# Causal attention with a gated LoRA branch on one core: minus the row maximum goes into the score bank ahead of the matmuls, output scaling moves to VectorE, and the jobs stand in another order

## The chip, the core and the metric

The program runs on one core of a Trainium2 chip. Five engines work in it, each with its own list of instructions, in order, tied together by semaphores: TensorE (PE, with the weight loads shown apart as PEld), VectorE (DVE), ScalarE (ACT), GpSimd (POOL) and SyncE (SP, which only issues DMAs here). The metric is the device time of one execution in microseconds (us), as the median of several runs.

## What is computed

The input x is 2048 tokens by 256. After a layer norm there are two branches, and the result is x + attention * silu(ffn). Everything is fp32.

```python
k, q, v = (einsum('ihd,bpd->biph', W, x) for W in (W_K, W_Q, W_V))   # 16 heads of 128
scores  = einsum('biph,biqh->biqp', k, q)                            # causal
masked  = scores * mask - 1e10 * (1 - mask)
attn    = softmax(masked / sqrt(128), axis=-1)
z       = einsum('biqp,biph->biqh', attn, v)
out     = einsum('df,bqf->bqd', W_O, z_flat)
# ffn: x W_base + b + 2 * (one of 8 LoRA experts, picked by argmax of a router)
```

## The kernel before

**Precision.** Each fp32 product is three matmuls in a fast fp32 form: hi*hi, hi*lo and lo*hi (`mm3`, lines 304 to 308). So every operand is held as a high part and a rest. The high part is written by ScalarE (a copy that rounds), the rest by VectorE (a subtraction).

**Tiling.** The queries of a head form 4 blocks of 512 (g = 0 to 3). A score tile is 128 keys by 512 queries, keys on the partitions. Block g has 4 (g + 1) such tiles, the last four of them on the diagonal and so 512, 384, 256 and 128 wide. That makes 40 tiles for a head, 80 for a pair of heads and 640 in all: 448 of the full width and 64 of each smaller width together with them (64 diagonal ones of full width are among the 448). Score banks in PSUM are used in turn, three of them; three more (`aux`) serve all other products.

**One tile.** PE computes the scores, adds the mask on a diagonal tile by one bf16 matmul (line 763), and then minus the row maximum is added. The maximum of a query is a number for each column of this layout, so it cannot be an activation's bias. There are two ways:

- a fourth matmul (line 765) of a matrix of ones with `shift`, a 128 x 512 tile in which POOL has put minus the maxima on diagonals (line 431);
- where `on_vector` is true (256 of the 640 tiles: blocks 2 and 3, not on the diagonal, five of six), a VectorE addition on the bank (line 620) of `negmax`, the same product made once for the block by the job Spread (a matmul at line 750 and a VectorE copy at line 610).

ScalarE then writes exp twice from the bank: `probs` (line 517) and its high part `p_hi` (line 518). VectorE writes `p_lo` (line 581). POOL sums the tiles into `colsum` (lines 456 to 463). PE multiplies with the values (the job Value).

**Row maxima.** For each block PE computes the scores a second time, the other way round and from the high parts alone (RowMax, line 745), 640 times; VectorE reduces each (lines 595 and 601), and then the four or more partial maxima (line 606).

**Output.** When a block's z is full, ScalarE and VectorE split it, PE takes the sums of the 512 queries (line 789) and multiplies with W_O (Out). ScalarE scales a 128 x 256 piece of that by 1 / sum into `scaled`, which is part of `gate` (line 527), and POOL adds it to `acc` (line 447). There are 256 such pieces.

**Order.** The order of all jobs is one list that the five engines share. A table `SCHEDULE` of 80 pieces, one for each score tile of a pair of heads, says which jobs follow that tile: P for a projection, V for a value projection, M for a RowMax, B for Spread, v or w for a Value, Z, S and O for the steps of the output. Each engine goes through the same list and takes its part of every job. SP loads the weights of the next head or pair once POOL has split the last ones (lines 347 to 376).

## Time and profile before

| what | number |
|---|---|
| median of 3 runs | 1572.15 us (1568.87 to 1574.76) |
| the profiled execution, its own time | 1567.74 us |
| its span (first to last instruction) | 1565.9 us |
| granted TensorE clock, mean | 0.986 of full speed |
| PE busy | 1507.5 us, 96% |
| DVE busy | 1297.8 us, 83% |
| POOL busy | 1118.6 us, 71% |
| ACT busy | 870.4 us, 56% |

Busy is the union of an engine's instructions. Matmuls are pipelined: the profile gives a 128 x 512 matmul some 0.4 us, while the next one starts 0.23 us after it. What a matmul takes from the engine is therefore read from the distance between two starts, not from its mean duration; the same is so, to a smaller extent, for ACT and DVE.

### The profile page before, as it was taken

To read this page: it belongs to the slowest core of one execution; us is meant where nothing else is said; L and a number is where in the kernel's file an instruction comes from. 1 tells how busy PE (TensorE), PEld (TensorE's weight loads), DVE (VectorE), ACT (ScalarE), POOL (GpSimd) and SP (SyncE) were. 2 spreads that over 40 slices of the span, in tenths; PEclk is the share of its full clock that TensorE was granted. 3 is DMA by queue.
4 is the path that set the end of the run, shared out by engine and by line. 5 is a ranking of instruction groups with operands and counts; after the bars stand their busy time and mean duration, and the time that the engine had idled before them with its cause. 6 is when DMAs were issued, how large, how long until landed. Compare 5 with 4: busy or idle time off the path is not lost.

```text
span 1565.9 us, 24075 instructions
## 1 busy us (share of the span) xinstructions
PE 1507.5 (96%) x8192; PEld 1271.6 (81%) x8192; DVE 1297.8 (83%) x2701; ACT 870.4 (56%) x1812; POOL 1118.6 (71%) x1010
## 2 busy tenths in 40 slices
PE   4999999999999999999999999999999999999987
PEld 3788878888888887888788888888888887888765
DVE  6788987889789796888978898897978989788864
ACT  2456555565555564566555655565655665566541
POOL 3468876687677786778866876778867788668860
PEclk9899999999999999999999999999999999999998
DMA  2000000000000000000000000000000000000002
GB/s 87 15 1 1 14 1 14 1 8 8 1 14 1 15 1 8 8 1 14 1 15 0 8 8 1 14 1 8 8 1 14 1 8 1 18 1 0 1 27 81
DMA packets 11640, 16.87 MB, mean 11 GB/s; under 512 B 768, under 2 KB 7424, under 8 KB 11520
## 3 DMA queue, kind: packets, MB, share of 16 engines
q1 hardware_dynamic: 11520, 15.35, 3.1%
q8 instruction: 66, 1.08, 0.3%
q14 instruction: 54, 0.44, 0.1%
HBM read 13.25 MB, written 2.10 MB: 10 GB/s over the span
## 4 chain that ended last, share of the span: by engine, by line
PE 76%; DVE 14%; POOL 5%; issue 3%; DMA 1%; ACT 0%; SPq 0%; POOLq 0%; DVEq 0%
PE ps L306 21%; PE ps L308 20%; PE ps L307 20%; DVE p_lo L581 7%; PE ps L745 6%; PE ps L765 4%; DVE ps L620 3%; PE ps L789 2%; DVE partmax L595 2%; POOL colsum L463 2%; PE ps L763 1%; POOL acc L447 1%; POOL shift L431 1%; POOL wo_hi L396 1%; POOL wo_lo L399 1%
## 5 line engine op out<-in xcount | busy, mean ns | idle before, releaser
L463 POOL TENSOR_TENSOR colsum<-colsum,probs 128x512 f32<-128x512 f32 (+3 forms) x512 | 628.8, 1228 | 194.6 <-ACT probs L517 158.6
L581 DVE TENSOR_TENSOR p_lo<-probs,p_hi 128x512 fp32r<-128x512 f32 (+3 forms) x640 | 589.6, 927 | 44.5 <-issue 31.7
L517 ACT ACTIVATE probs<-ps 128x512 f32<-128x512 f32 (+3 forms) x640 | 342.8, 536 | 481.7 <-PE ps L765 252.3
L518 ACT ACTIVATE p_hi<-ps 128x512 fp32r<-128x512 f32 (+3 forms) x640 | 339.8, 531 | 0.0
L447 POOL TENSOR_TENSOR acc<-acc,gate 128x256 f32<-128x256 f32 x256 | 235.0, 938 | 86.1 <-ACT gate L527 85.2
L595 DVE TENSOR_REDUCE partmax<-ps 128x1 f32<-128x512 f32 x384 | 250.4, 679 | 22.9 <-PE ps L745 22.8
L306 PE MATMUL ps<-qT_hi,kT_hi 128*128 128x512 f32 (+3 forms) x640 | 236.1, 369 | 0.0
L306 PE MATMUL ps<-p_hi,v_hi 128*128 128x512 f32 (+3 forms) x640 | 232.9, 364 | 2.7 <-DVE p_lo L581 2.7
L745 PE MATMUL ps<-kT_hi,qT_hi 128*128 128x512 f32 (+3 forms) x640 | 224.8, 378 | 10.9 <-DVE partmax L595 8.9
L308 PE MATMUL ps<-qT_hi,kT_lo 128*128 128x512 f32 (+3 forms) x640 | 234.3, 366 | 0.0
L307 PE MATMUL ps<-qT_lo,kT_hi 128*128 128x512 f32 (+3 forms) x640 | 234.3, 366 | 0.0
L307 PE MATMUL ps<-p_lo,v_hi 128*128 128x512 f32 (+3 forms) x640 | 232.9, 364 | 0.0
L308 PE MATMUL ps<-p_hi,v_lo 128*128 128x512 f32 (+3 forms) x640 | 232.8, 364 | 0.0
L620 DVE TENSOR_TENSOR ps<-ps,negmax 128x512 f32<-128x512 f32 x256 | 176.5, 689 | 17.4 <-PE ps L308 14.7
L745 PEld LDWEIGHTS ps<-kT_hi,qT_hi 128*128 128x128 f32 x640 | 121.2, 191 | 43.7 <-DVE partmax L595 23.2
L765 PE MATMUL ps<-shift,ones_r 128*128 128x512 f32 (+3 forms) x384 | 152.2, 396 | 0.0
L306 PEld LDWEIGHTS ps<-p_hi,v_hi 128*128 128x128 f32 x640 | 121.3, 189 | 20.3 <-DVE p_lo L581 5.4
L308 PEld LDWEIGHTS ps<-qT_hi,kT_lo 128*128 128x128 f32 x640 | 121.1, 189 | 19.6
L459 POOL TENSOR_TENSOR colsum<-probs 128x384 f32<-128x384 f32 (+1 forms) x64 | 78.3, 1223 | 81.3 <-ACT probs L517 81.3
L308 PEld LDWEIGHTS ps<-p_hi,v_lo 128*128 128x128 f32 x640 | 120.6, 188 | 18.9
L307 PEld LDWEIGHTS ps<-qT_lo,kT_hi 128*128 128x128 f32 x640 | 121.1, 189 | 17.1
L527 ACT ACTIVATE gate<-ps,rinv 128x256 f32<-128x256 f32 x256 | 109.4, 475 | 45.0 <-PE ps L308 39.0
(114 smaller groups left out, 2636.4 us busy)
## 6 DMA issues: line engine op xcount, KB each, us to landing
wraw<-wqk_dram SPq DMA_DIRECT2D x16, 256.0 KB, 2.6
acc<-x_dram SPq DMA_DIRECT2D x4, 512.0 KB, 7.3
wraw<-wv_dram SPq DMA_DIRECT2D x8, 256.0 KB, 2.7
wraw<-wo_dram SPq DMA_DIRECT2D x8, 256.0 KB, 2.7
probs<-x_dram SPq DMA_DIRECT2D x4, 512.0 KB, 4.6
out_dram<-acc SPq DMA_DIRECT2D x4, 512.0 KB, 3.1
wraw<-ffn_w_dram SPq DMA_DIRECT2D x2, 196.0 KB, 2.4
wraw<-lora_b_dram SPq DMA_DIRECT2D x1, 128.0 KB, 2.7
```

The source lines that it names most:

```text
L306: nc.tensor.matmul(dst, w_hi, m_hi, start=first, stop=False)
L307: nc.tensor.matmul(dst, w_hi, m_lo, start=False, stop=False)
L308: return nc.tensor.matmul(dst, w_lo, m_hi, start=False, stop=last)
L447: nc.gpsimd.tensor_tensor(dst, dst, scaled[:, k, :], ALU.add).then_inc(out_added, 1)
L463: nc.gpsimd.tensor_tensor(total[:, c0:], total[:, c0:], tile[:, c0:], ALU.add)\
L517: nc.scalar.activation(probs[:, k, c0:], src, ACT.Exp, scale=SCALE).then_inc(probs_ready, 1)
L518: nc.scalar.activation(p_hi[:, k, c0:], src, ACT.Exp, scale=SCALE).then_inc(hi_ready, 1)
L581: nc.vector.tensor_tensor(p_lo[:, k, c0:], probs[:, k, c0:], f32(p_hi[:, k, c0:]), ALU.subtract)\
L595: nc.vector.reduce_max(dst, src, axis=AX).then_inc(aux_free, 1)
L620: nc.vector.tensor_tensor(bank, bank, negmax[:, job.g - 2, :], ALU.add)\
L745: nc.tensor.matmul(dst[:, 0:w], qT_hi[:, job.g, job.q * P:(job.q + 1) * P], kT_hi[:, k_slot(job.head, job.c), 0:w], start=True, stop=True)\
L765: op = nc.tensor.matmul(dst, ones_r[:, :], shift[:, job.g, :, :].rearrange("p t n -> p (t n)")[:, c0:], start=False, stop=True)
```

## The change

The three ways in which minus the maximum reached the scores are gone (`shift` on POOL, the matmuls at lines 750 and 765, the VectorE addition at line 620 and the copy at line 610). In their place:

- SP writes a block's `rowmax` (128 x 4) to DRAM and reads it back as one row of 512 on all 128 partitions, `maxrow`. Each of the two DMAs is waited for. The second also waits until the same block of the head before has used up its `maxrow`. SP now goes through the shared list, with the weight loads between these.
- ScalarE writes `-maxrow` into the score bank two tiles ahead (`seed`), and PE's three matmuls add to it (`start=False`). For that the banks' accumulate marks are set once by 12 matmuls at the start. PE's wait on the exp of three tiles before is replaced by a wait for the seed.
- The row that arrives is in the order 4 p + t, so the seed reads it with a step of four floats.
- VectorE scales and adds an output piece in one instruction; ScalarE and POOL have no part in it any more.
- `SCHEDULE` is another table.

```diff
-            def make_shift(job, block_no):
-                pool.wait_ge(max_ready, block_no)
-                k = job.g
-                nc.gpsimd.tensor_tensor(
-                    shift[:, k, :, :], neg_ident[:, None, :].broadcast_to([P, TB, P]),
-                    rowmax[:, k, :][:, :, None].broadcast_to([P, TB, P]), ALU.mult).then_inc(shift_ready, 1)
...
+                if isinstance(job, RowMax) and job.last:
+                    blocks += 1
+                    row = max_dram[job.head * NB + job.g]
+                    sp.wait_ge(max_ready, blocks)
+                    sp.dma_start(row.rearrange("(p t) -> p t", t=TB), rowmax[:, job.g, :]).then_inc(max_out, 16)
+                    sp.wait_ge(max_out, 16 * blocks)
+                    if job.head:
+                        sp.wait_ge(seeded, tiles_until((job.head - 1) * NB + job.g))
+                    sp.dma_start(maxrow[:, job.g, :], row.partition_broadcast(P)).then_inc(max_spread[job.g], 16)
...
+            def seed(job):
+
+                if job.n >= SCORE_BANKS:
+                    act.wait_ge(hi_ready, job.n - SCORE_BANKS + 1)
+                if job.kt == 0:
+                    act.wait_ge(max_spread[job.g], 16 * (job.head + 1))
+                q = columns(job) // P
+                nc.scalar.activation(st[job.n % SCORE_BANKS].rearrange("p (t n) -> p t n", t=TB)[:, q:, :],
+                                     maxrow[:, job.g, :].rearrange("p (n t) -> p t n", t=TB)[:, q:, :],
+                                     ACT.Copy, scale=-1.0).then_inc(seeded, 1)
...
                     nc.scalar.activation(probs[:, k, c0:], src, ACT.Exp, scale=SCALE).then_inc(probs_ready, 1)
                     nc.scalar.activation(p_hi[:, k, c0:], src, ACT.Exp, scale=SCALE).then_inc(hi_ready, 1)
-                elif isinstance(job, Out):
...
+                    if n + SEED_AHEAD < len(scores):
+                        seed(scores[n + SEED_AHEAD])
...
-                    if on_vector(job):
...
-                        dve.wait_ge(scores_ready, job.n + 1)
-                        nc.vector.tensor_tensor(bank, bank, negmax[:, job.g - 2, :], ALU.add)\
-                          .then_inc(shifted, 1)
...
+                        op = nc.vector.scalar_tensor_tensor(
+                            dst, aux[job.aux % AUX_BANKS][:, k * D:(k + 1) * D],
+                            rinv[:, job.gi % 2, q:q + 1], dst, ALU.mult, ALU.add)
+                    op.then_inc(aux_free, 1)
...
+            for bank in st:
+                for q in range(TB):
+                    op = nc.tensor.matmul(bank[:, q * P:(q + 1) * P], ones_r[:, :], ones_r[:, :], start=q == 0,
+                                          stop=True, skip_group_check=True)
+            op.then_inc(bits_set, 1)
...
-                    if job.kt == 0:
-                        pe.wait_ge(shift_ready, job.head * NB + job.g + 1)
-                    if n >= SCORE_BANKS:
-                        pe.wait_ge(hi_ready, n - SCORE_BANKS + 1)
+                    pe.wait_ge(seeded, n + 1)
...
-                    if not on_vector(job):
-                        op = nc.tensor.matmul(dst, ones_r[:, :],
-                                              shift[:, job.g, :, :].rearrange("p t n -> p (t n)")[:, c0:],
-                                              start=False, stop=True)
...
-    "V11 w | w V01 V00 | w | Pk02 Pq03 V10 v z7 s7 | "
+    "V00 w Pq03 V01 w w z7 | | Pk02 | s7 Pk03 v V11 | o70 v M0222 | M0212 o71 v M0202 M0232 v | V21 S0 Z0 | v V10 "
...
```

**TensorE, around two narrow diagonal tiles.** Names: `ps<-qT_hi,kT_hi` and the two rows after it are a score tile, `ps<-mask_bf,ident_bf` the mask, `ps<-shift,ones_r` minus the maximum, `ps<-kT_hi,qT_hi` a RowMax, `ps<-p_hi,v_hi` and the two after it a Value. Before, in block 1 of an odd head:

```order
L306 MATMUL ps<-qT_hi,kT_hi 128x256 [waits hi_ready]
L307 MATMUL ps<-qT_lo,kT_hi 128x256
L308 MATMUL ps<-qT_hi,kT_lo 128x256
L763 MATMUL ps<-mask_bf,ident_bf 128x128
L765 MATMUL ps<-shift,ones_r 128x256
L306 MATMUL ps<-p_hi,v_hi 128x512 [waits lo_ready]
L307 MATMUL ps<-p_lo,v_hi 128x512
L308 MATMUL ps<-p_hi,v_lo 128x512
L745 MATMUL ps<-kT_hi,qT_hi 128x512 [waits aux_free] x2
```

The same tile of the same kind of block now, from the end of the tile before it (384 wide) to the start of the one after it (128 wide):

```order
L731 MATMUL ps<-mask_bf,ident_bf 128x128
L719 MATMUL ps<-kT_hi,qT_hi 128x512 [waits aux_free]
L281 MATMUL ps<-qT_hi,kT_hi 128x256 [waits seeded]
L282 MATMUL ps<-qT_lo,kT_hi 128x256
L283 MATMUL ps<-qT_hi,kT_lo 128x256
L731 MATMUL ps<-mask_bf,ident_bf 128x128
L281 MATMUL ps<-p_hi,v_hi 128x512 [waits lo_ready]
L282 MATMUL ps<-p_lo,v_hi 128x512
L283 MATMUL ps<-p_hi,v_lo 128x512
L281 MATMUL ps<-qT_hi,kT_hi 128x128 [waits seeded]
```

The matmul of ones with `shift` is gone, the tile waits for `seeded`, and the jobs between two tiles are others.

**ScalarE, at the same place.** `probs` and `p_hi` are the two exps of a tile, `kT_hi` and `z_hi` copies for other jobs, `gate` the scaling of an output piece, `ps<-maxrow` a seed. Before:

```order
L506 ACTIVATE kT_hi<-ps 128x512 [waits aux_full]
L517 ACTIVATE probs<-ps 128x512 [waits sum_done,scores_ready]
L518 ACTIVATE p_hi<-ps 128x512
L517 ACTIVATE probs<-ps 128x384 [waits sum_done,scores_ready]
L518 ACTIVATE p_hi<-ps 128x384
L527 ACTIVATE gate<-ps,rinv 128x256 [waits out_added,aux_free,aux_full]
L527 ACTIVATE gate<-ps,rinv 128x256 [waits out_added]
```

Now:

```order
L486 ACTIVATE kT_hi<-ps 128x512 [waits aux_full]
L498 ACTIVATE probs<-ps 128x384 [waits sum_done,scores_ready]
L499 ACTIVATE p_hi<-ps 128x384
L478 ACTIVATE ps<-maxrow 128x128 [waits hi_ready]
L498 ACTIVATE probs<-ps 128x256 [waits sum_done,scores_ready]
L499 ACTIVATE p_hi<-ps 128x256
L478 ACTIVATE ps<-maxrow 128x512 [waits max_spread2,hi_ready]
L498 ACTIVATE probs<-ps 128x128 [waits sum_done,scores_ready]
```

Every tile has a third instruction, which fills the bank of the tile two further on; the first tile of a block also waits for the DMA there. The scalings of outputs are gone.

**VectorE, just before that place.** `ps<-ps,negmax` is the addition to a score bank, `acc<-ps,rinv,acc` the new scaling and adding. Before:

```order
L620 TENSOR_TENSOR ps<-ps,negmax 128x512 [waits scores_ready]
L581 TENSOR_TENSOR p_lo<-probs,p_hi 128x512 [waits hi_ready]
L595 TENSOR_REDUCE partmax<-ps 128x1 [waits aux_full] x2
L638 MEMSET wait_slot 128x1 [waits out_scaled]
L581 TENSOR_TENSOR p_lo<-probs,p_hi 128x512 [waits hi_ready]
```

Now:

```order
L566 TENSOR_REDUCE partmax<-ps 128x1 [waits aux_full]
L551 TENSOR_TENSOR p_lo<-probs,p_hi 128x512 [waits hi_ready]
L603 SCALAR_TENSOR_TENSOR acc<-ps,rinv,acc 128x256 [waits aux_free,aux_full]
L603 SCALAR_TENSOR_TENSOR acc<-ps,rinv,acc 128x256
L551 TENSOR_TENSOR p_lo<-probs,p_hi 128x512 [waits hi_ready]
```

VectorE no longer stands between PE and ScalarE in any tile, and has two new instructions for each output job.

## Rows read from the trace of the kernel before

**Rows 1.** The page's busy times: busy us, share, count.
```profile
PE 1507.5 (96%) x8192; PEld 1271.6 (81%) x8192; DVE 1297.8 (83%) x2701; ACT 870.4 (56%) x1812; POOL 1118.6 (71%) x1010
```

**Rows 2.** Busy time by stretch: length, PE, PEld, DVE, ACT, POOL, clock, DMA.
```profile
80.00:1500.00 1420.00, 1398.82 (x7669) 1185.45 (x7668) 1211.87 (x2494) 827.46 (x1734) 1072.07 (x947) 1.00 0.02 6
```

**Rows 3.** Waits of the whole span: us in total, times, longest.
```profile
PEld ps L745 <- DVE partmax L595: 23.2, 38, 1.0
PE ps L750 <- POOL shift L431: 10.5, 8, 3.0
PE ps L745 <- DVE partmax L595: 8.9, 16, 0.7
```

**Rows 4.** PE in order of time: start, duration; width 512.
```profile
702.88 0.40 PE L765 MATMUL ps<-shift,ones_r 128*128 128x512 f32 x1
703.12 0.40 PE L306 MATMUL ps<-xT_hi,wqk_hi 128*128 128x512 f32 x1
```

**Rows 5.** The same, around a diagonal tile of width 256.
```profile
773.64 0.28 PE L308 MATMUL ps<-qT_hi,kT_lo 128*128 128x256 f32 x1
773.76 0.23 PE L763 MATMUL ps<-mask_bf,ident_bf 128*128 128x128 bf16 x1
773.80 0.36 PE L765 MATMUL ps<-shift,ones_r 128*128 128x256 f32 x1
774.00 0.39 PE L745 MATMUL ps<-kT_hi,qT_hi 128*128 128x512 f32 x1
```

**Rows 6.** Groups of instructions by shape: count, busy us, mean ns, idle before.
```profile
L581 DVE TENSOR_TENSOR p_lo<-probs,p_hi 128x512 fp32r<-128x512 f32 x448 | 447.3, 1000 | 40.1 <-issue 27.4 <-ACT p_hi L518 12.7
L447 POOL TENSOR_TENSOR acc<-acc,gate 128x256 f32<-128x256 f32 x256 | 235.0, 938 | 86.1 <-ACT gate L527 85.2
L620 DVE TENSOR_TENSOR ps<-ps,negmax 128x512 f32<-128x512 f32 x256 | 176.5, 689 | 17.4 <-PE ps L308 14.7
L527 ACT ACTIVATE gate<-ps,rinv 128x256 f32<-128x256 f32 x256 | 109.4, 475 | 45.0 <-PE ps L308 39.0 <-POOL acc L447 2.8
L431 POOL TENSOR_TENSOR shift<-neg_ident,rowmax 128x512 fp32r<-128x512 f32 x64 | 84.7, 1323 | 13.3 <-DVE rowmax L606 12.7
L765 PE MATMUL ps<-shift,ones_r 128*128 128x512 f32 x192 | 82.6, 430 | 0.0
L601 DVE CUSTOM_DVE_ANT_0 gate<-ps,mask_rows 128x256 f32<-128x256 f32 x64 | 26.6, 416 | 2.3 <-issue 2.3
L610 DVE COPY negmax<-ps 128x512 f32<-128x512 f32 x32 | 21.8, 682 | 4.0 <-PE ps L750 4.0
L750 PE MATMUL ps<-shift,ones_r 128*128 128x512 f32 x32 | 13.2, 414 | 10.5 <-POOL shift L431 10.5
```

**Rows 7.** The same view, the high part's exp on ACT, widest and narrowest.
```profile
L518 ACT ACTIVATE p_hi<-ps 128x512 fp32r<-128x512 f32 x448 | 266.4, 595 | 0.0
...
L518 ACT ACTIVATE p_hi<-ps 128x128 fp32r<-128x128 f32 x64 | 18.0, 281 | 0.0
```

**Rows 8.** ACT in order of time.
```profile
706.72 0.60 ACT L517 ACTIVATE probs<-ps 128x512 f32<-128x512 f32 x1 [0.45 <-PE ps L765]
707.21 0.59 ACT L518 ACTIVATE p_hi<-ps 128x512 fp32r<-128x512 f32 x1
```

**Rows 9.** DVE in order of time.
```profile
733.05 0.68 DVE L581 TENSOR_TENSOR p_lo<-probs,p_hi 128x512 fp32r<-128x512 f32 x1
...
734.43 1.26 DVE L581 TENSOR_TENSOR p_lo<-probs,p_hi 128x512 fp32r<-128x512 f32 x1
```

**Rows 10.** POOL in the same stretch.
```profile
733.85 2.99 POOL L463 TENSOR_TENSOR colsum<-colsum,probs 128x512 f32<-128x512 f32 x2 [0.69 <-ACT probs L517]
```

**Rows 11.** DMA issues of the page: count, KB each, median us to landing.
```profile
wraw<-wqk_dram SPq DMA_DIRECT2D x16, 256.0 KB, 2.6
wraw<-bias_dram SPq DMA_DIRECT2D x1, 128.0 KB, 3.5
```

More of the change, by code:

```diff
@@ L34 @@
 SCORE_BANKS = 3
+SEED_AHEAD = 2
 AUX_BANKS = 3
@@ L48 @@
 Normed = namedtuple("Normed", "aux ev c b")
-Spread = namedtuple("Spread", "aux head g")
 Base = namedtuple("Base", "b")
@@ L60, in number @@
             ev += 1
-        elif kind in (RowMax, Spread, Sums, Out):
+        elif kind in (RowMax, Sums, Out):
             plan.append(kind(aux, *args))
@@ L153, in follow @@
                 which = (code[1], head) if what == "P" else (head,)
-                kinds.append(({"P": Project, "M": RowMax, "B": Spread}[what], (*which, *digits[1:])))
+                kinds.append(({"P": Project, "M": RowMax}[what], (*which, *digits[1:])))
     for n, step in enumerate(steps):
@@ L162, in plan_program @@
     return number(mark_last(kinds))
-def on_vector(score):
-    return score.g >= 2 and score.kt < TB * score.g and score.kt % 6 > 0
 def attention_layer(nc, x, wqk, wv, wo, ffn_w, lora_b, bias, out):
@@ L283, in k_slot @@
             return NB + b if head % 2 and b < 2 else b
-        shifts_before = [0]
-        for job in plan:
-            if isinstance(job, Score):
-                shifts_before.append(shifts_before[-1] + on_vector(job))
-        SLOTS = 2
-        def tiles_out(job):
-            return job.gi * TB + 2 * job.half
+        scores = [job for job in plan if isinstance(job, Score)]
         def columns(t):
@@ L362, in _, with weights @@
-            for i in range(PAIRS - 1):
-                loads(i, False)
-            loads(PAIRS - 1, True)
-            sp.wait_ge(wqk_ready, H)
-            sp.wait_ge(wv_ready, PAIRS)
-            sp.wait_ge(wo_ready, PAIRS)
-            for c in range(DC):
-                sp.dma_start(wraw[:, c, 0:FW], ffn_w[:, c, :]).then_inc(ffn_in, 16)
-            sp.dma_start(wraw[:, 2, 0:D], lora_b).then_inc(ffn_in, 16)
-            sp.dma_start(wraw[:, 2, D:2 * D], bias.partition_broadcast(P)).then_inc(ffn_in, 16)
+            def weights(raw, src, nth, ready, count, arrived):
+                sp.wait_ge(ready, count)
+                sp.dma_start(wraw[:, raw, :], src[:, nth, :]).then_inc(arrived, 16)
@@ new lines, in ffn_weights @@
+            def ffn_weights():
+                sp.wait_ge(wqk_ready, H)
+                sp.wait_ge(wv_ready, PAIRS)
+                sp.wait_ge(wo_ready, PAIRS)
+                for c in range(DC):
+                    sp.dma_start(wraw[:, c, 0:FW], ffn_w[:, c, :]).then_inc(ffn_in, 16)
+                sp.dma_start(wraw[:, 2, 0:D], lora_b).then_inc(ffn_in, 16)
+                sp.dma_start(wraw[:, 2, D:2 * D], bias.partition_broadcast(P)).then_inc(ffn_in, 16)
+            blocks = 0
+            for job in plan:
+                if isinstance(job, RowMax) and job.last:
[7 more added lines that the diff above has]
+                    sp.dma_start(maxrow[:, job.g, :], row.partition_broadcast(P)).then_inc(max_spread[job.g], 16)
+                if not isinstance(job, Score):
+                    continue
+                i, at, last = job.n // TILES, job.n % TILES, job.n // TILES == PAIRS - 1
+                if at == 0:
+                    weights(0, wqk, 2 * i + 1, wqk_ready, 2 * i + 1, wqk_in)
+                if at == 1 and not last:
+                    weights(1, wv, i + 1, wv_ready, i + 1, wv_in)
+                if at == 10 and not last:
+                    weights(2, wo, i + 1, wo_ready, i + 1, wo_in)
+                if at == 12 and not last:
+                    weights(0, wqk, 2 * i + 2, wqk_ready, 2 * i + 2, wqk_in)
+                if at == 12 and last:
+                    ffn_weights()
@@ L499, in _ @@
             nc.scalar.activation(rstd[:, 1, :], rstd[:, 0, :], ACT.Sqrt).then_inc(sqrt_done, 1)
-            sums_aux = {job.gi: job.aux for job in plan if isinstance(job, Sums)}
+            def seed(job):
[7 more added lines that the diff above has]
+                                     ACT.Copy, scale=-1.0).then_inc(seeded, 1)
             for job in plan:
@@ L509, in _ @@
                     k = n % PROBS
-                    if on_vector(job):
-                        act.wait_ge(shifted, shifts_before[n] + 1)
-                    else:
-                        act.wait_ge(scores_ready, n + 1)
+                    if n == 0:
+                        act.wait_ge(bits_set, 1)
+                        for ahead in scores[:SEED_AHEAD]:
+                            seed(ahead)
+                    act.wait_ge(scores_ready, n + 1)
                     if n >= PROBS:
@@ L582, in lo_part @@
                   .then_inc(lo_ready, 1)
-            waiting, spread_out = [], None
+            sums_aux = {job.gi: job.aux for job in plan if isinstance(job, Sums)}
+            waiting = []
             for job in plan:
```

95 lines of the change are left out of this document (26 added, 69 removed), and 22 rows, old and new, of the table SCHEDULE.

## The prediction, made before the changed kernel was run

> **What bounds the kernel now.** I read the page's busy times first, then the busy times by stretch, then the waits, and then PE in order of time. The busy times put PE at 1507.5 of 1565.9 us, with DVE at 83%, POOL at 71% and ACT at 56% [rows 1]. Between 80 and 1500 us, which is nearly all of the work on the 640 tiles, PE is idle for 1420 - 1398.82 = 21.2 us [rows 2]. So PE is the bound, and a matmul less is time less, as long as nothing new makes PE wait. The waits show who makes it wait today: the Spread matmul for POOL's `shift`, 10.5 us, and RowMax matmuls for VectorE to empty an `aux` bank, 8.9 us on PE and 23.2 us on its weight loads [rows 3].
>
> How long a matmul holds PE has to be read between two starts. The matmul with `shift` starts at 702.88 and the next one at 703.12: 0.24 us, with a duration of 0.40 [rows 4]. Over many such pairs I use 0.233. For a diagonal tile of width 256 the score matmul takes 773.76 - 773.64 = 0.12, the mask 0.04, and the matmul with `shift` 774.00 - 773.80 = 0.20 [rows 5], which is 0.08 more than its width. I put these 0.08 down to the bf16 mask ahead of it, so they stay with the mask.
>
> **What goes from PE.** The matmuls at line 765: 192 of full width at 0.233, 44.7 us [count in rows 6], and 64 each of 384, 256 and 128 columns. For 256 I take 0.12 [rows 5], for 384 the middle between 0.12 and 0.233, 0.176, for 128 half of 0.12: 64 x (0.176 + 0.12 + 0.06) = 22.8 us. The 32 at line 750: 32 x 0.233 = 7.5 us [rows 6]. Together 75.0 us. If the 0.08 went too, on 256 diagonal tiles, it would be 20.5 us more. The durations of the same groups (82.6 us for the 192 alone) would make it nearly twice as much; they overlap, and I do not use them. The 12 matmuls at the start are issued while PE has nothing to multiply yet: its first work is a transpose that needs the layer norm. Cost 0.
>
> The Spread job goes, and with it the wait for POOL, 10.5 us [rows 3]. What is late next there? Nothing on PE: the maxima now come to ScalarE.
>
> **What goes from and comes to VectorE.** It loses 176.5 us (line 620) and 21.8 us (line 610) [rows 6]. It gets 256 pieces of 128 x 256, from PSUM and SBUF to SBUF. No such instruction is in the trace. The nearest row is the masked maximum of the same size, which also reads one operand from each: 0.416 [rows 6], so 106 us; the lower bound is half of a 512-wide one, 256 x 0.34 = 88, the upper one the p_lo rate of a 512-wide one halved, 256 x 0.5 = 128. Net -92 us. There is a second gain that the diff does not name. `p_lo` takes 0.68 us where POOL is idle and 1.26 us where POOL's sum stands beside it [rows 9, 10]; its mean is 1.00 [rows 6]. That is (1.00 - 0.68) x 448 = 143 us of waiting for POOL. POOL loses 235.0 and 84.7 us [rows 6] of its 1118.6, 29%, so some 0.29 x 143 = 41 us of it should go. VectorE falls from 1298 to about 1165 us, still some 79% of a shorter span. Since it is quicker, the waits of RowMax for an `aux` bank should shrink. Of 8.9 us and 23.2 us of late weight loads [rows 3] I take 6 us as gain; bounds 0 and 20.
>
> **What comes to ScalarE.** 640 seeds, from SBUF to PSUM. The nearest row is `p_hi` of the same size: 0.595 us for 512 columns, 0.281 for 128 [rows 7], so 266.4 + 18.0 and two widths between, about 340 us; back to back the next instruction starts 0.49 us after (706.72 to 707.21) [rows 8], which makes the lower bound about 0.8 of that, 275 us. It loses 109.4 us (line 527) [rows 6]. ScalarE ends between 870 - 109 + 275 = 1036 and 1101 us, under 75% of the new span. As a sum this fits. The seed's step of four floats is in no row of this trace. The upper bound is the slowest elementwise row of 512 columns, POOL's 1.32 [rows 6].
>
> Here a rule speaks against the change. The rows say nothing of a strided read on ScalarE. The Trainium skill, "SBUF — State Buffer", section on the DMA ports, says that SBUF has 16-byte lines, that full rate needs at least two accesses in a row to the same line, and that each access to a new line pays. A step of four floats touches a new line with each element. The page gives no price; no run here shows it yet. It is the first rival below.
>
> **Does the seed make PE wait?** Before, a tile waited for the exp of the third tile before it. Now it waits for its seed, which stands behind the exp of the second tile before it. From the end of one tile's scores to the start of the tile after the next, ScalarE must do two exps and a seed: the start of the first is 0.2 us behind (the pipelined end), then 0.49 + 0.49 + 0.60 = 1.8 us in all. What PE does in that time stands in the order. The tightest full-width places have only a Value job in each of the two gaps: 3 + 3 + 3 matmuls, 9 x 0.233 = 2.1 us, 0.3 to spare. The tightest narrow place is the one shown of PE: a RowMax 0.23, three matmuls of 256 at 0.12 and the mask with its 0.12, a Value 0.70, together 1.4; ScalarE needs 0.2 + two exps of 384 and a seed of 128. By the durations between 0.6 and 0.28 that is 0.2 + 0.4 + 0.4 + 0.28 = 1.3. So room everywhere, with very little in ten or so of the 80 pieces, and an average of about 3 us. Behind the seed stand the copies and exps of the next tiles, for which VectorE and PE wait; several tight tiles in a row leave ScalarE behind by some tenths. I take 1 us for each of the 8 pairs of heads, 8 us; bounds 0 and 40.
>
> **Are the maxima there in time?** From the last RowMax of a block: VectorE empties its queue and reduces, about 1.5 us, a DMA of 2 KB, a DMA of 256 KB. The weight loads of 256 KB land after 2.6 us, the broadcast of the bias after 3.5 [rows 11]. I take 2.6 + 3.5 and 0.5 us for each issue, 8.6 us in all. In the new table the last RowMax stands 5 to 12 tiles ahead of the block's first tile, and at the tightest places (six tiles, or seven, with little between) the matmuls of the pieces between add up to 9.3 to 10.6 us. POOL's `shift` took 1.3 us for that [rows 6] with four or five tiles. It fits, by 1 or 2 us. ScalarE can be held up ahead of that seed for a moment with its next exp behind it; that is in the 8 us.
>
> **The sum.** 1565.9 - 75.0 - 10.5 - 6 + 8 = 1482.4 us of span. The profiled execution took 1.8 us more than its span, and the median of the runs was 4.4 us above the profiled one: 1488.6, say 1488.
>
> **Rivals.**
> - *Slow seeds.* If the strided read runs at half the rate of the elements, a full seed takes 0.60 + 512 x (0.595 - 0.281) / 384 = 1.02 us. ScalarE then needs 2.2 us where the tight places give 1.9 to 2.1, eleven of 80 by the order: 88 x 0.25 = 22 us directly, and its load goes to 1101 + 190 = 1290 us, 85%, with queues behind it for as much again: 1535. For: no row has the access. Against: nothing but the page's rule.
> - *Very slow seeds, slower than before.* ScalarE becomes the bound once it would be busy for more than about 90% of 1566 us, that is 1410 us, of which 761 are its other work: 650 us of seeds, or 1.15 us for a full one. At POOL's 1.32 the full seeds make 591 us and the narrow ones about 150: 761 + 741 = 1502 us busy, and with the idle ends and 7% of waiting in order about 1640. It is slower from 1.15 us a seed.
> - *The maxima come late.* The way through DRAM needs to take 11 us instead of 8.6: then the tight blocks, two or three of eight in a pair, wait 1 to 2 us each, 8 x 2.5 x 1.5 = 30 us more: 1518. To be slower than before it would need 13 us.
> - *More is won.* The 0.08 behind each mask go with the `shift` matmul (20.5 us) and half of the late weight loads too (10 us more): 1457.
> - *The change does not do what it says* would be the case if the accumulate marks cost something on each tile; the same three matmuls run in both, so I give it nothing of its own.
>
> **How the numbers follow.** My forecast, 1488 with its own range 1465 to 1515: 0.66. More is won, 1457: 0.12. Slow seeds, 1535: 0.08. Late maxima, 1518: 0.06. Very slow seeds, 1640: 0.08. The rule on lines bears on the two kinds of slow seeds; it carries half of their 0.16. Half a per cent is what runs of this kernel can tell from no change. Faster takes the first four but for a fifth of the slow seeds: 0.90; within half a per cent 0.02; slower 0.08. The range for 8 in 10 is 1452 to 1535.
>
> **What would show it.** Right: PE starts after a score tile without the `shift` matmul, PE still over 93% busy, its distances between starts unchanged; seeds of 0.6 us; few waits of PE for ACT's seed; `p_lo` near 0.91 in the mean; VectorE near 1165 us. Wrong: a group of waits of PE on the seeds or of ACT on the maxima's DMA of tens of us; a seed above 0.9 us; diagonal tiles whose next matmul starts without the 0.08.

## The result: 1.4% faster, a quarter of the forecast

| | median us | runs |
|---|---|---|
| before | 1573.45 | 1568.87 to 1578.76 |
| after | 1548.33 | 1547.73 to 1548.76 |

The ratio is 0.9863, with an interval of 0.9824 to 0.9903 (the two medians of the table alone give 0.984). The gain is clear of the noise and under 2%. The forecast was 1488 us, with a range of 1452 to 1535, so the measured time lies above the range.

The changed kernel's page, first the busy times, which answer to [rows 1], then the chain that ended last by engine:

```profile
span 1546.2 us, 23204 instructions
...
PE 1459.5 (94%) x7788; PEld 1193.2 (77%) x7788; DVE 1248.1 (81%) x2541; ACT 1274.0 (82%) x2196; POOL 793.4 (51%) x688
...
PE 51%; ACT 24%; DVE 13%; issue 9%; POOL 2%; DMA 0%; SPq 0%; ACTq 0%; POOLq 0%; DVEq 0%
```

The same chain in the kernel before:

```profile
PE 76%; DVE 14%; POOL 5%; issue 3%; DMA 1%; ACT 0%; SPq 0%; POOLq 0%; DVEq 0%
```

ScalarE is at 1274 us, where I had 1036 to 1101, and has a quarter of the chain; before it had none of it. PE lost 404 matmuls, and is idle more. The middle stretch (length, then PE, PEld, DVE, ACT, POOL, clock) answers to [rows 2]:

```profile
80.00:1480.00 1400.00, 1345.26 (x7215) 1102.61 (x7214) 1158.51 (x2319) 1212.15 (x2094) 753.70 (x635) 1.00 0.08 18
```

PE is idle for 54.7 of 1400 us, against 21.2 of 1420. That is not all the time it stands late: a 512-wide matmul counts as busy for 0.40 us while the next can start after 0.23, so a short delay hides in the busy time. Counted by starts instead (each matmul at the median distance to the next for its width, those behind a mask apart), the matmuls themselves fall from 1457.0 to 1386.4 us, and what is left of the span rises from 108.9 to 159.8 us. Groups of instructions by shape (busy us, mean ns, idle before) show why:

```profile
L478 ACT ACTIVATE ps<-maxrow 128x512 f32<-128x512 f32 x448 | 517.5, 1155 | 8.9 <-DMA maxrow<-max_dram 8.7
L551 DVE TENSOR_TENSOR p_lo<-probs,p_hi 128x512 fp32r<-128x512 f32 x448 | 509.3, 1141 | 42.1 <-ACT p_hi L499 41.1
...
L603 DVE SCALAR_TENSOR_TENSOR acc<-ps,rinv,acc 128x256 f32<-128x256 f32 x256 | 111.3, 475 | 13.0 <-PE ps L283 12.1
```

A full seed takes 1.155 us. In order of time, ScalarE with the seed between its neighbours, which answers to [rows 8]:

```profile
700.61 0.61 ACT L499 ACTIVATE p_hi<-ps 128x512 fp32r<-128x512 f32 x1
701.08 1.14 ACT L478 ACTIVATE ps<-maxrow 128x512 f32<-128x512 f32 x1
702.10 0.63 ACT L504 ACTIVATE z_hi<-ps 128x512 fp32r<-128x512 f32 x1
```

The exp holds ScalarE for 701.08 - 700.61 = 0.47 us, the seed for 1.02. The waits, which answer to [rows 3], have new names:

```profile
PEld ps L281 <- ACT ps L478: 46.5, 106, 1.2
...
PEld ps L281 <- DVE partmax L566: 32.6, 31, 1.9
...
PEld ps L281 <- DVE p_lo L551: 25.1, 40, 1.3
PE ps L281 <- DVE partmax L566: 22.6, 23, 1.5
...
PE ps L281 <- DVE p_lo L551: 12.2, 16, 1.0
...
PE ps L281 <- ACT ps L478: 9.6, 32, 0.8
...
ACT ps L478 <- DMA maxrow<-max_dram: 8.7, 3, 8.2
```

Only part of the idle time names the seed. The rest names VectorE: what ScalarE hands on late (`p_hi`, the copies for `qT`, `kT`, `v` and z) VectorE finishes late, and PE waits there (read from the waits here; e13 below, where only the seed differs, bears it out). A slow engine that stands two steps back shows under the name of the step between.

### The profile page after: what moved, and what is told of

It reads as the page before. It is cut to its first block, busy times and chain, and to the rows that moved or that the text cites. A ratio compares the mean times of both kernels' runs of the same rounds, so it can differ in the third digit from the quotient of the medians.

```text
span 1546.2 us, 23204 instructions
## 1 busy us (share of the span) xinstructions
PE 1459.5 (94%) x7788; PEld 1193.2 (77%) x7788; DVE 1248.1 (81%) x2541; ACT 1274.0 (82%) x2196; POOL 793.4 (51%) x688
## 4 chain that ended last, share of the span: by engine, by line
PE 51%; ACT 24%; DVE 13%; issue 9%; POOL 2%; DMA 0%; SPq 0%; ACTq 0%; POOLq 0%; DVEq 0%
PE ps L281 15%; PE ps L282 14%; PE ps L283 14%; ACT ps L478 7%; ACT probs L498 7%; ACT p_hi L499 6%; DVE p_lo L551 6%; PE ps L719 4%; DVE partmax L566 3%; POOL colsum L433 2%; PE ps L754 2%; ACT qT_hi L486 1%; DVE z_lo L588 1%; ACT z_hi L504 1%; PE ps L731 1%
## 5 line engine op out<-in xcount | busy, mean ns | idle before, releaser
L433 POOL TENSOR_TENSOR colsum<-colsum,probs 128x512 f32<-128x512 f32 (+3 forms) x512 | 610.2, 1192 | 388.3 <-ACT probs L498 373.6
L478 ACT ACTIVATE ps<-maxrow 128x512 f32<-128x512 f32 (+3 forms) x640 | 645.3, 1008 | 8.9 <-DMA maxrow<-max_dram 8.7
L551 DVE TENSOR_TENSOR p_lo<-probs,p_hi 128x512 fp32r<-128x512 f32 (+3 forms) x640 | 614.9, 968 | 42.4 <-ACT p_hi L499 41.4
L498 ACT ACTIVATE probs<-ps 128x512 f32<-128x512 f32 (+3 forms) x640 | 362.9, 567 | 141.4 <-PE ps L731 74.8
L499 ACT ACTIVATE p_hi<-ps 128x512 fp32r<-128x512 f32 (+3 forms) x640 | 365.3, 571 | 0.0
L566 DVE TENSOR_REDUCE partmax<-ps 128x1 f32<-128x512 f32 x384 | 256.9, 679 | 10.4 <-PE ps L719 9.5
L281 PE MATMUL ps<-qT_hi,kT_hi 128*128 128x512 f32 (+3 forms) x640 | 247.6, 387 | 12.7 <-ACT ps L478 9.6
L281 PE MATMUL ps<-p_hi,v_hi 128*128 128x512 f32 (+3 forms) x640 | 241.7, 378 | 13.2 <-DVE p_lo L551 12.2
L281 PEld LDWEIGHTS ps<-qT_hi,kT_hi 128*128 128x128 f32 x640 | 121.5, 190 | 60.6 <-ACT ps L478 46.5
L282 PEld LDWEIGHTS ps<-p_lo,v_hi 128*128 128x128 f32 x640 | 121.1, 189 | 14.8
L572 DVE CUSTOM_DVE_ANT_0 gate<-ps,mask_rows 128x384 f32<-128x384 f32 (+3 forms) x256 | 121.5, 483 | 8.6 <-issue 8.6
```

The lines of the kernel that those rows point to most:

```text
L281: nc.tensor.matmul(dst, w_hi, m_hi, start=first, stop=False, skip_group_check=seed)
L282: nc.tensor.matmul(dst, w_hi, m_lo, start=False, stop=False, skip_group_check=seed)
L433: nc.gpsimd.tensor_tensor(total[:, c0:], total[:, c0:], tile[:, c0:], ALU.add)\
L478: nc.scalar.activation(st[job.n % SCORE_BANKS].rearrange("p (t n) -> p t n", t=TB)[:, q:, :], maxrow[:, job.g, :].rearrange("p (n t) -> p ...
L498: nc.scalar.activation(probs[:, k, c0:], src, ACT.Exp, scale=SCALE).then_inc(probs_ready, 1)
L499: nc.scalar.activation(p_hi[:, k, c0:], src, ACT.Exp, scale=SCALE).then_inc(hi_ready, 1)
```

## The experiments

Theory A: the seed is slow because of its stepped read, and that keeps the time at 1548. Rival B: reading SBUF and writing PSUM is slow in itself. Rival C: the new table, or VectorE's meetings with POOL, holds the time. Rival D: lighter VectorE and POOL bring a part of the gain. The first three are as they stood before e1 to e4; D was added with the second group, e5 to e8. All ratios are to the kernel before on the same chip; a kernel executed once has none. The chips of the four groups (e1 to e4, e5 to e8, e9 to e12, e13 and e14) differ, and the kernel before had medians of 1567.8 to 1577.0 us on them, so differences of less than some 10 us between groups mean little.

| run | what | us | ratio, interval |
|---|---|---|---|
| e1 | read without a step, DRAM written in 4-byte runs | 1791.2 | 1.1402 (1.1320 to 1.1484) |
| e2 | read with a step of two on full tiles | 1449.8 | one execution |
| e3 | seed of four columns | 1448.0 | 0.9242 (0.9187 to 0.9298) |
| e4 | e1 with the old table | 1903.2 | 1.2125 (1.2053 to 1.2197) |
| e5 | 8-byte runs, step of two | 1448.3 | 0.9197 (0.9145 to 0.9249) |
| e6 | put in order once a block | 1482.0 | 0.9410 (0.9350 to 0.9469) |
| e7 | e2 with the old table | 1518.4 | 0.9648 (0.9581 to 0.9714) |
| e8 | e2, outputs back on ScalarE and POOL | 1527.9 | 0.9700 (0.9624 to 0.9777) |
| e9 | before, outputs on VectorE | 1579.6 | 1.0040 (1.0020 to 1.0059) |
| e10 | before, new table | 1642.7 | 1.0443 (1.0409 to 1.0478) |
| e11 | before, both of these | 1599.2 | 1.0167 (1.0128 to 1.0207) |
| e12 | the step on the write | 1453.4 | one execution |
| e13 | straight read, scattered write | 1449.8 | 0.9241 (0.9211 to 0.9271) |
| e14 | e13 with POOL's sums cut short | 1439.3 | 0.9173 (0.9138 to 0.9208) |

### e1: the read without a step, paid for by the DMA

```diff
-                    sp.dma_start(row.rearrange("(p t) -> p t", t=TB), rowmax[:, job.g, :]).then_inc(max_out, 16)
+                    sp.dma_start(row.rearrange("(t p) -> p t", p=P), rowmax[:, job.g, :],
+                                 allow_slow_non_contiguous=True).then_inc(max_out, 16)
...
+                nc.scalar.activation(st[job.n % SCORE_BANKS][:, c0:], maxrow[:, job.g, c0:],
                                      ACT.Copy, scale=-1.0).then_inc(seeded, 1)
```

> The DMA that writes a block's maxima puts them into DRAM in the order of the score tile, so that the seed reads maxrow without a step; the write becomes 512 elements of 4 bytes in place of 128 runs of 16. Nothing else changes. Theory A (the step of four floats is what makes a full seed take 1.155 us and leaves ScalarE at 82%): a full seed falls to about 0.6 us, ScalarE's busy time by 640 x 0.4 = 230 us to about 1040 us, PE's waits for the seeds to near 0, and the time to about 1500 us, near the 1488 of the forecast. Rival B (reading SBUF and writing PSUM is what is slow, whatever the step): the seed stays at 1.1 us and the time within 5 us of 1548. Rival C (the new table or VectorE's meetings with POOL hold the time): the seed gets short but the time stays above 1535 us.

The time was a miss: 1791 us. By its letter that is rival C's case (a short seed and over 1535 us), but not by its cause, as the waits show. Its groups of instructions and its waits (total, times, longest), SP's among them:

```profile
L479 ACT ACTIVATE ps<-maxrow 128x512 f32<-128x512 f32 x448 | 274.3, 612 | 297.5 <-DMA maxrow<-max_dram 297.5
```

```profile
SPq L346 <- DMA max_dram<-rowmax: 533.2, 63, 10.5
```

The same wait in the changed kernel:

```profile
SPq L345 <- DMA max_dram<-rowmax: 90.7, 64, 2.9
```

The seed is 0.612 us, so rival B is out. But the write of 2 KB in 512 runs of 4 bytes takes 533.2 / 63 = 8.5 us where 128 runs of 16 took 1.4, and ScalarE waits 297.5 us for the maxima. I had named the write in the expectation and not priced it.

### e2 and e3: short seeds without that

In e2 the 448 full tiles read with a step of two floats:

```diff
...
+                nc.scalar.activation(st[job.n % SCORE_BANKS].rearrange("p (t n) -> p t n", t=2),
+                                     maxrow[:, job.g, :].rearrange("p (n t) -> p t n", t=2),
                                      ACT.Copy, scale=-1.0).then_inc(seeded, 1)
```

In e3 a seed is four columns:

```diff
...
+                nc.scalar.activation(st[job.n % SCORE_BANKS][:, c0:c0 + 4], maxrow[:, job.g, c0:c0 + 4],
                                      ACT.Copy, scale=-1.0).then_inc(seeded, 1)
```

> The seeds of the 448 full tiles read maxrow with a step of two floats, so that two accesses in a row fall into the same 16 bytes; narrow seeds keep the step of four. The maxima then land on the wrong queries, which is the part of the computation that changes. Theory A in the form of the skill's rule (two accesses for each 16-byte line give full rate): full seeds take about 0.6 us. If the price rises with each step away from contiguous: about 0.8 to 0.9 us. Rival B: 1.1 us as before.

> The seed writes four columns and no more, so the maxima are not subtracted from the rest; every wait and every other instruction stays. It shows what is left when the seeds cost ScalarE nearly nothing: a seed of about 0.2 us. Theory A: the time falls to 1470 to 1490 us, and a contiguous seed of full size stays within 15 us of that. Rival C: it stays above 1530 us, since ScalarE was not what counted.

In e2:

```profile
L483 ACT ACTIVATE ps<-maxrow 128x512 f32<-128x512 f32 x448 | 294.1, 657 | 8.8 <-DMA maxrow<-max_dram 8.7
...
L479 ACT ACTIVATE ps<-maxrow 128x384 f32<-128x384 f32 x64 | 56.8, 887 | 0.0
```

Two floats of each 16 bytes bring nearly all of it: 0.657 us. In the same kernel the narrow seeds, still with a step of four, take 0.887 us for fewer columns. The time falls by 99 us, to what nearly free seeds give (e3, 1448.0). Theory A had expected 1470 to 1490 us of e3, so its mechanism was met and its size was not: 22 us more is won than it allowed. So theory A holds for the cause: with seeds of 0.6 us the kernel has nothing more to gain from them, and rival C as the holder of the time is out.

### e4 and e7: the old table

```diff
-    "V00 w Pq03 V01 w w z7 | | Pk02 | s7 Pk03 v V11 | ...
+    "V11 w | w V01 V00 | w | Pk02 Pq03 V10 v z7 s7 | ...
```

> As the contiguous kernel, but with the table of job order of the kernel before, without its Spread entries. It shows what the new table is worth once the seeds are short. If the new table fits the new dependences (seed two tiles ahead, VectorE with the output pieces): this is 10 to 30 us slower than the contiguous one. If the table costs (rival C): this one is faster, by 10 us or more. In the old table the maxima of some blocks come only 4 tiles ahead, so waits of ScalarE for the DMA of up to 1 to 3 us in some 16 to 24 blocks should appear, 20 to 50 us in all.

> The kernel with the step of two floats on full tiles (the maxima land on the wrong queries), with the table of job order of the kernel before. With the new table it took 1450 us. Theory A with my sum (75 us of matmuls and 10 us of waits): the old table gives about 1485 us, and the 35 us to 1450 are the new table's. Rival D (the 35 us come from VectorE and POOL having less to do): the old table gives 1450 to 1465 us as well.

Both are slower with the old table: e4 by 112 us against e1, where 10 to 30 were expected, and e7 by 69 us against e2, twice the 35 that were expected. In e4 the DMA's waits, with the slow write of e1, make up most: ScalarE waits 426.5 us for the maxima, 129 more than in e1. Rival D alone cannot explain it. e7's seeds:

```profile
L494 ACT ACTIVATE ps<-maxrow 128x512 f32<-128x512 f32 x448 | 293.8, 656 | 93.0 <-DMA maxrow<-max_dram 93.0
```

The old table leaves less time between a block's last RowMax and its first tile, and ScalarE waits 93 us for the DMA.

### e5, e6 and e13: three ways to the right result

e5 writes the maxima in 256 runs of 8 bytes and reads with a step of two:

```diff
-                    sp.dma_start(row.rearrange("(p t) -> p t", t=TB), rowmax[:, job.g, :]).then_inc(max_out, 16)
+                    sp.dma_start(row.rearrange("(h p t) -> p h t", h=2, t=2), rowmax[:, job.g, :].rearrange("p (h t) -> p h t", h=2)).then_inc(max_out, 16)
...
+                    src = maxrow[:, job.g, :].rearrange("p (h n t) -> p h t n", h=2, t=2)
...
```

> The same result as the changed kernel. The maxima go to DRAM in pairs: 256 runs of 8 bytes in place of 128 runs of 16, and the seed then reads them with a step of two floats. The seed is short (0.61 to 0.66 us for a full one by the two runs before). What is open is the write: 16-byte runs landed after 1.4 us, 4-byte ones after about 8. If the time goes by the number of runs, this one takes 3 to 4 us, the maxima are late in few blocks, and the kernel takes 1450 to 1480 us. If it goes by something that already costs in full at 8 bytes, it takes 6 us or more and the time is above 1550 us.

e6 puts each block's row in order once, into SBUF, and waits for that:

```diff
+                    nc.scalar.activation(maxcol[:, job.g % 2, :].rearrange("p (t n) -> p t n", t=TB),
+                                         maxrow[:, job.g, :].rearrange("p (n t) -> p t n", t=TB),
+                                         ACT.Copy, scale=-1.0).then_inc(ordered, 1)
+                    act.wait_ge(ordered, job.head * NB + job.g + 1)
...
```

> The same result as the changed kernel. ScalarE reads maxrow with the step of four floats once for a block, 64 times in all, and writes it in the order of the tile into a buffer in SBUF; the 640 seeds read that without a step. The DMA is as in the changed kernel. Theory A (the step is the cost): seeds of 0.6 us, ScalarE busy 1040 + 64 x 1.1 = 1110 us, the time 1450 to 1465 us. Against it would be a time above 1500 us. It also keeps the DMA's 1.4 us, so it has no late maxima.

e13 turns the patterns round: the read goes straight through memory, the write to PSUM has an inner step of 128 floats:

```diff
-                nc.scalar.activation(st[job.n % SCORE_BANKS].rearrange("p (t n) -> p t n", t=TB)[:, q:, :],
-                                     maxrow[:, job.g, :].rearrange("p (n t) -> p t n", t=TB)[:, q:, :],
+                nc.scalar.activation(st[job.n % SCORE_BANKS].rearrange("p (t n) -> p n t", t=TB)[:, :, q:],
+                                     maxrow[:, job.g, :].rearrange("p (n t) -> p n t", t=TB)[:, :, q:],
                                      ACT.Copy, scale=-1.0).then_inc(seeded, 1)
```

> The same result as the changed kernel, and the same two DMAs. The seed reads maxrow without a step, in the order 4 p + t, and writes each number where it belongs in the bank: the inner step of the write to PSUM is 128 floats. Theory A in its last form (only the read from SBUF pays for a step): full seeds of 0.61 us, ScalarE near 1030 us busy, 1443 to 1455 us. If only the write step of four was free and one of 128 is not: seeds of 1 us or more and above 1520 us.

The page of e5 has the two DMAs (count, KB, us to landing):

```profile
maxrow<-max_dram SPq DMA_DIRECT2D x64, 256.0 KB, 3.9
...
max_dram<-rowmax SPq DMA_DIRECT2D x64, 2.0 KB, 3.1
```

So 16-, 8- and 4-byte runs take 1.4, 3.1 and 8.5 us. e5 is at 1448.3, just under the 1450 to 1480 that were expected for a write of 3 to 4 us. e6 was 17 us above its expected upper end: 64 stepped copies of 1.137 us and, behind each, a wait before the seed can start, just where a block begins; PE's weight loads wait 33.8 us for seeds, against 3.8 in e13.

e13, its busy times, its middle stretch and its seeds:

```profile
PE 1412.2 (98%) x7788; PEld 1197.3 (83%) x7788; DVE 1200.7 (83%) x2541; ACT 1037.0 (72%) x2196; POOL 847.4 (59%) x688
```

```profile
80.00:1382.00 1302.00, 1297.61 (x7205) 1105.22 (x7204) 1108.63 (x2318) 981.78 (x2090) 805.59 (x635) 1.00 0.08 19
```

```profile
L478 ACT ACTIVATE ps<-maxrow 128x512 f32<-128x512 f32 x448 | 276.3, 617 | 10.9 <-DMA maxrow<-max_dram 10.8
...
L551 DVE TENSOR_TENSOR p_lo<-probs,p_hi 128x512 fp32r<-128x512 f32 x448 | 463.7, 1042 | 12.6 <-ACT p_hi L499 12.2
```

With two patterns exchanged, the same data and the same DMAs, a full seed falls from 1.155 to 0.617 us and PE is idle for 4.4 of 1302 us. By starts, the matmuls take 1382.4 us and what is left of the span is 65.4, against 159.8 in the changed kernel: 94 of the 98 us between the two spans are time in which PE stood late. e5 and e13 (intervals 0.9145 to 0.9249 and 0.9211 to 0.9271) are not told apart. Both compute what the changed kernel computes and are faster than either kernel of the case; e13 is the smaller edit.

### e12: the step on the write

```diff
...
+                nc.scalar.activation(st[job.n % SCORE_BANKS].rearrange("p (n t) -> p t n", t=TB)[:, q:, :],
+                                     maxrow[:, job.g, :].rearrange("p (t n) -> p t n", t=TB)[:, q:, :],
                                      ACT.Copy, scale=-1.0).then_inc(seeded, 1)
```

> The changed kernel, with the seed turned round: it reads maxrow without a step and writes the bank in PSUM with a step of four floats (the maxima land on the wrong queries; narrow tiles are filled at other columns than they use). It tells whether the step costs only on the read from SBUF. If it is the 16-byte line of SBUF alone: seeds of 0.61 us and 1450 us. If a step costs on the PSUM side as well: seeds of 1 us or more and about 1550 us.

Its full seeds:

```profile
L478 ACT ACTIVATE ps<-maxrow 128x512 f32<-128x512 f32 x448 | 276.1, 616 | 9.5 <-DMA maxrow<-max_dram 9.2
```

The time is 1453.4 us. A step of four floats on the PSUM side costs nothing that shows; with e13, neither does one of 128.

### e8 to e11: the other parts, alone and together

e8 is e2 with the old way of the outputs; e9 is the kernel before with the new one:

```diff
-                    dve.wait_ge(out_scaled, tiles_out(job) + 2)
-                    nc.vector.memset(wait_slot[:, job.aux % AUX_BANKS:job.aux % AUX_BANKS + 1], 0.0)\
-                      .then_inc(aux_free, 1)
+                    dve.wait_ge(aux_full, job.aux + 1)
...
+                        op = nc.vector.scalar_tensor_tensor(
+                            dst, aux[job.aux % AUX_BANKS][:, k * D:(k + 1) * D],
+                            rinv[:, job.gi % 2, q:q + 1], dst, ALU.mult, ALU.add)
+                    op.then_inc(aux_free, 1)
```

> As the kernel with the step of two floats, new table, but an output piece is scaled by ScalarE and added by POOL, as in the kernel before. If the move to VectorE brings something (rival D), this is 10 to 40 us slower than 1450 us, with longer p_lo, since POOL's 235 us come back. If it brings nothing: 1450 us within 5, since PE was not waiting for either.

> The kernel before with one part of the change alone: VectorE scales and adds the output pieces, ScalarE and POOL have no part in them. The same result. By the run with the outputs moved back (78 us slower in the new order) one would expect 20 us or more of gain here too. By the sum of the forecast (VectorE gets 106 us of work for 8 us of memsets while it still adds the maxima to 256 banks, so it is at about 89%) it is no gain: between 10 us faster and 20 us slower, with more waits of PE for VectorE.

e10 is the kernel before with the new table and its Spread entries; e11 has e9's and e10's edits:

```diff
-    "V11 w | w V01 V00 | w | Pk02 Pq03 V10 v z7 s7 | ...
+    'V00 w Pq03 V01 w w z7 | | Pk02 | ... | M0311 O00 v v M0303 B02 | ...
```

> The kernel before with the new table alone, and the four Spread entries put in three tiles behind the last RowMax of their block. The same result. If the new table is the better order in itself, this is 10 to 40 us faster than 1572. If it only fits the new way of the maxima and the lighter POOL and VectorE, it is as fast or slower, since in it one tile has up to six jobs behind it and the next one none.

> The kernel before with the new table and the outputs on VectorE, but with the maxima as before (matmul with shift, Spread, VectorE's addition). The same result. What is left from here to 1450 us is the way of the maxima: 71 us of matmuls on PE and VectorE's additions. If the parts only add up, this one takes about 1450 + 71 + 10 = 1530 us; if VectorE, now at 89%, is what holds it, it takes 1560 us or more.

| | old table | new table |
|---|---|---|
| maxima as before, outputs as before | 1573.45 (before) | 1642.7 (e10) |
| maxima as before, outputs on VectorE | 1579.6 (e9) | 1599.2 (e11) |
| maxima by short seeds, outputs as before | not run | 1527.9 (e8) |
| maxima by short seeds, outputs on VectorE | 1518.4 (e7) | 1449.8 (e2) |

No part outside the seeds gains anything alone: the outputs on VectorE cost 0.4%, the table 4.4%, both 1.7%. e9 was expected between 10 us faster and 20 slower by one argument and 20 or more faster by the other; the first held. But the parts need each other. In the new table the outputs on VectorE are worth 43 us without seeds (e11 against e10) and 78 us with short ones (e8 against e2); on top of short seeds and these outputs the table is worth 69. Both of the last are more than was expected. e11 took the high branch of its expectation (1560 us or more) and lies 69 us above the sum of the parts (1530): they do not add up.

What holds e8 stands in its waits:

```profile
PEld ps L742 <- DVE wait_slot L628: 30.1, 33, 1.9
...
DVE wait_slot L628 <- ACT gate L529: 22.1, 25, 1.5
ACT gate L529 <- POOL acc L430: 21.9, 25, 2.7
```

PE waits for an `aux` bank that VectorE may free only after ScalarE has scaled the piece, and ScalarE waits for POOL's addition of the last one. That this path makes up the 78 us is read from the waits, not tried alone. e11's busy times and chain:

```profile
PE 1520.7 (95%) x8192; PEld 1260.1 (79%) x8192; DVE 1351.6 (85%) x2829; ACT 760.9 (48%) x1556; POOL 863.5 (54%) x754
...
PE 63%; DVE 29%; issue 4%; ACT 3%; DMA 1%; POOL 0%; SPq 0%; DVEq 0%; ACTq 0%; POOLq 0%
```

VectorE has 29% of the chain. In 256 tiles PE, VectorE's addition, ScalarE's exp and VectorE's `p_lo` stand in a row, and the new table, with up to three Values and several RowMax behind one tile and nothing behind the next, gives VectorE uneven work. That e10 and e11 are slower for just this reason was argued from the chain and the waits, not tried alone, and the share of the chain is no measure of it: e9 has 39% there and loses 0.4% only.

### e14: POOL's sums cut short

```diff
-                    nc.gpsimd.tensor_tensor(total[:, c0:], total[:, c0:], tile[:, c0:], ALU.add)\
+                    nc.gpsimd.tensor_tensor(total[:, c0:c0 + 4], total[:, c0:c0 + 4], tile[:, c0:c0 + 4], ALU.add)\
                       .then_inc(sum_done, 1)
...
```

> As that kernel, but POOL's sums take four columns of a tile in place of all (the softmax sums are wrong for the rest). POOL's busy time falls from 850 to under 350 us and it hardly meets VectorE. Expected: p_lo of a full tile falls from 1.04 to 0.70 us, VectorE's busy time by some 150 us. If the forecast's gain from a lighter POOL had a ground in time, the kernel gets 10 us or more faster than the one before it; if PE is the bound in the middle of it anyway, the time stays within 5 us.

```profile
PE 1407.1 (98%) x7788; PEld 1198.0 (83%) x7788; DVE 1028.5 (72%) x2541; ACT 1036.7 (72%) x2196; POOL 255.4 (18%) x689
```

```profile
L552 DVE TENSOR_TENSOR p_lo<-probs,p_hi 128x512 fp32r<-128x512 f32 x448 | 309.1, 694 | 37.4 <-ACT p_hi L500 36.6
```

`p_lo` falls to 0.694 us and VectorE by 172 us, but the kernel by 10.5 us only. That is just inside the branch in which the lighter POOL has a ground in time (10 us or more), and small against VectorE's 172 because PE was the bound already: 98% busy in both.

## Why the prediction was wrong, step by step

**The seed's price: the step that failed.** I took ScalarE as 1036 to 1101 us and a full seed as 0.595 us, from "the nearest row", `p_hi` of the same size. It was 1.155, and 1274 us. The stepped read was named as the one property that no row showed, and it was given 0.16. The Trainium skill, "SBUF — State Buffer", section on the DMA ports, has the rule of 16-byte lines with two accesses a line for full rate. By that rule, the trace agrees in each case that was run: one float of each line 1.155 us, two 0.657, four 0.612 to 0.617. Two are 0.04 us short of four, which the rule does not give. The difference between e13 and the changed kernel is the price of that one step: 1548.3 - 1449.8 = 98.5 us. The forecast missed by 60 us and not by 98 because it was short by 38 us on the other side, on PE's waits below. With seeds of the price that I took, the time is 1449.8 us, and that too is outside the range, under its lower end of 1452.

**The point from which slow seeds lose.** The rival of half the element rate gave 1.02 us and 1535; the one from 1.15 us on gave slower than before. Measured: 1.155 us and 1548, still faster. I had added durations where ScalarE's instructions overlap. Between starts a seed takes 1.02 us, and ScalarE ends at 82% busy, not at the 90% of my bound. The mechanism of the rival of half the rate was right, late banks and queues behind them, but that its 1535 comes near is luck: it added 47 us for the slow seeds to 1488, and they cost 98.5 on top of 1449.8.

**The matmuls.** 75 us, with 0.08 left behind the mask. Right: by starts, the matmuls themselves take 74.6 us less in e13 than before (1457.0 and 1382.4), and 70.6 less in the changed kernel. The 0.08 stays: in the changed kernel the matmul after the mask is another job's (a RowMax, a Value, a projection), and a full-width one holds PE for 0.31 us, as the `shift` matmul did, for which [rows 5] show the same at 256 columns. PE in order of time (start, us), one RowMax that is not behind a mask and one that is:

```profile
707.00 0.39 PE L719 MATMUL ps<-kT_hi,qT_hi 128*128 128x512 f32 x1
707.22 0.33 PE L281 MATMUL ps<-qT_hi,kT_hi 128*128 128x384 f32 x1
...
707.75 0.23 PE L731 MATMUL ps<-mask_bf,ident_bf 128*128 128x128 bf16 x1
707.79 0.47 PE L719 MATMUL ps<-kT_hi,qT_hi 128*128 128x512 f32 x1
708.10 0.28 PE L281 MATMUL ps<-qT_hi,kT_hi 128*128 128x256 f32 x1
```

The first holds PE for 707.22 - 707.00 = 0.22 us, the second for 708.10 - 707.79 = 0.31. Over all pairs of mask and a 512-wide RowMax the distance after the RowMax starts has a median of 0.314 us (62 pairs), against 0.314 for the 64 `shift` matmuls of full width.

**PE's waits.** I took 10.5 us of Spread waits and 6 us of others as gain, and 8 us of new ones. With short seeds PE's idle time in the middle falls from 21.2 to 4.4 us, and weight loads of a RowMax wait 3.7 us for VectorE where it was 23.2 [rows 3]. By starts, all the time of the span that is not matmuls falls from 108.9 to 65.4 us, by 43.5, where my three terms come to 8.5. So the forecast was short on this side: 1449.8 against 1488. The table of the experiments says what this hangs on, but does not divide it: with short seeds the new table is worth 69 us (against e7, which has 93 us of waits for the maxima) and the outputs on VectorE are worth 78, each more than the whole shortfall, and neither gains alone. I had treated the table as something that could cost a few us, and had no term for what the two gain together.

**The lighter POOL.** Wrong. I scaled the time `p_lo` loses to POOL by POOL's load and took 41 us off. POOL's load fell by 29%, and `p_lo` rose from 1.00 to 1.141 us in the changed kernel and 1.042 in e13. Both follow the exps of the same tile: POOL's sum starts when `probs` is there, `p_lo` half a microsecond later, in the middle of it. What went from POOL was other work: in the kernel before 305 of the 448 full `p_lo` stand beside a sum into `colsum`, in e13 385. Two runs test the load by itself: e8 puts POOL's additions back (841.5 to 1060.6 us busy) and a full `p_lo` goes from 1.069 to 1.083 us only; e9 takes them from the kernel before (1118.6 to 888.4) and it goes from 1.000 to 1.026. e14 shows the meetings are real, 0.35 us for each full tile, and worth 10.5 us.

**The new VectorE instruction.** 0.475 us against 0.416 taken (range 0.34 to 0.5): 111.3 us against 106.

**The maxima in time.** Right. I took 2.6 us for the small write (1.4) and 3.5 for the broadcast (3.8); ScalarE waits 8.7 us for them in all. e1 and e7 show how near that is: 8.5 us for the write costs 340 us (a part of it by the clock, see below), and the old table costs 93 us of waits.

## What to carry to other kernels

When an operation is moved to another engine, price its access pattern, not only its size; where no row has the pattern, put the step on the side whose cost is known, or try it alone first. A wait does not fall with an engine's load if both sides are set off by the same event. A hand-made order and the dependences it was made for are one change: taken apart, each of the two can lose what they gain together.

## What the runs showed of the hardware

- ScalarE, 128 x 512 fp32 from SBUF to PSUM: 0.612 us without a step, 0.657 with a read step of 8 bytes, 1.155 with one of 16 bytes. A write step of 16 or of 512 bytes in PSUM: 0.616 and 0.617.
- A 2 KB DMA write to DRAM from 128 partitions: 1.4 us in 16-byte runs, 3.1 in 8-byte runs, 8.5 in 4-byte runs.
- VectorE beside POOL, e13: a 128 x 512 `p_lo`, both operands in SBUF, takes 0.687 us in the 47 cases with no POOL instruction beside it and 1.084 in the mean of the other 401. The same operation with one operand in PSUM (`qT_lo`, `kT_lo`) takes 0.69 us at most, whether POOL works or not.
- A matmul behind the bf16 mask holds PE for 0.314 us at 512 columns, where others hold it for 0.23.
- In e1, where PE waits for seeds that wait for the maxima, the granted clock of the middle stretch is 0.92, 1.00 in e13, and PE's same 7200 matmuls there are 1411 us busy against 1298. The clock stands at the lower of its two levels (1.2 GHz) for 301 us of e1's span and for 19 of e13's. In the middle stretch of e1 it falls 43 times, and ahead of each fall stands a wait of PE of 1.7 to 10.4 us; two full-width matmuls are then 0.427 us apart and not 0.231. So e1's 341 us over e13 hold a share for the clock beside PE's 235.7 us of waits for seeds. The middle stretch of e1:

```profile
80.00:1724.00 1644.00, 1411.06 (x7244) 1189.27 (x7243) 1120.67 (x2332) 985.72 (x2105) 800.29 (x640) 0.92 0.08 16
```
